# TensorE: the high-part multiplications of a group first, then the low-part ones

## The reference

```
inputs = emb[feature_ids] * feature_vals[:, :, None]          # (1024, 39, 16)
h = inputs
for i in range(3):
    x = einsum('bhd,bmd->bhmd', h, inputs).reshape(B, -1, 16)  # every h times every field
    x = relu(einsum('bcd,oc->bod', x, Ws[i]) + bs[i])          # 200 outputs
    h, direct = (x[:, :100], x[:, 100:]) if i != 2 else (None, x)
    finals.append(direct)
d = relu(relu(inputs.reshape(B, -1) @ dnn_W0.T + dnn_b0) @ dnn_W1.T + dnn_b1)
out = concat(sum(finals, axis=-1), d) @ fc_W.T + fc_b + sum(bias_emb[feature_ids] * feature_vals)
```

## Time and profile before

| | |
|---|---|
| median of 3 runs | 2750.92 us (2747.41 to 2753.69) |
| profiled execution, its own time | 2752.34 us |
| its span, first to last instruction | 2750.5 us |
| TensorE matmul busy | 2649.5 us, 96% of the span |
| TensorE weight load busy | 2640.2 us, 96% |
| VectorE, GpSimd, ScalarE busy | 83%, 82%, 67% |

### The profile page before, as it was taken

The page is one execution under the profiler, slowest core; times in us unless marked ns, Lnnn a source line. Parts: engine busy times, 40 slices in busy tenths (PEclk is TensorE's granted clock), DMA queues, the critical chain, the costliest instruction groups (busy, mean ns, idle before and its releaser), DMA issues.

```text
span 2750.5 us, 66670 instructions
## 1 busy us (share of the span) xinstructions
PE 2649.5 (96%) x17928; PEld 2640.2 (96%) x17928; DVE 2285.0 (83%) x4584; ACT 1834.6 (67%) x4776; POOL 2249.6 (82%) x1912
## 2 busy tenths in 40 slices
PE   0699999999999999999999999999999999999999
PEld 0599999999999999999999999999999999999998
DVE  2788888888888888888888888888888888888884
ACT  0576776766767667676777767677677766766663
POOL 6788888888888888888888888888888888877763
PEclk9799999999999999999999999999999999999999
DMA  8844545445444454544545455454554545545441
GB/s 149 199 124 123 133 126 130 124 118 144 116 133 125 118 149 112 136 121 122 146 111 138 120 131 137 114 136 118 138 131 118 133 117 140 129 117 136 111 115 51
DMA packets 199914, 349.82 MB, mean 127 GB/s; under 512 B 66632, under 2 KB 118697, under 8 KB 199615
## 3 DMA queue, kind: packets, MB, share of 16 engines
q1 hardware_dynamic: 185782, 342.81, 45.6%
q0 software_dynamic: 10496, 2.88, 3.1%
q10 hardware_dynamic: 3464, 2.68, 0.3%
HBM read 344.29 MB, written 14.17 MB: 130 GB/s over the span
## 4 chain that ended last, share of the span: by engine, by line
PE 94%; POOL 2%; SPq 2%; DVE 1%; issue 1%; DMA 1%; ACT 0%; POOLq 0%; ACTq 0%; DVEq 0%
PE acc L642 61%; PE acc L643 28%; PE acc L667 2%; POOL raw L498 1%; PE hrep L678 1%; DVE W L1061 0%; SPq L319 0%; DMA odd<-lin 0%; PE acc L742 0%; PE acc L743 0%; PE acc L744 0%; SPq L309 0%; DMA raw<-table,idx 0%; PE hrep L764 0%; PE hrep L766 0%
## 5 line engine op out<-in xcount | busy, mean ns | idle before, releaser
L642 PE MATMUL acc<-W,xhi_d 128*128 128x400 f32 x5632 | 1732.4, 367 | 17.2 <-DVE xlo_d L1087 10.6
L643 PE MATMUL acc<-W,xlo_d 128*128 128x200 f32 x5632 | 1434.9, 255 | 0.0
L1087 DVE TENSOR_TENSOR xlo_d<-prod_d,xhi_d 128x512 fp32r<-128x512 f32 (+1 forms) x1536 | 983.9, 641 | 205.1 <-ACT xhi_d L819 147.2
L1079 DVE TENSOR_TENSOR prod_d<-hrep,xrep 128x512 f32<-128x512 f32 (+1 forms) x1536 | 1039.0, 677 | 105.8 <-issue 27.7
L548 POOL TENSOR_TENSOR xlo_p<-prod_p,xhi_p 128x512 fp32r<-128x512 f32 (+1 forms) x768 | 953.8, 1242 | 181.3 <-ACT xhi_p L813 135.6
L642 PEld LDWEIGHTS acc<-W,xhi_d 128*128 128x128 f32 x5632 | 1059.9, 188 | 20.1 <-DVE xlo_d L1087 12.9
L643 PEld LDWEIGHTS acc<-W,xlo_d 128*128 128x128 f32 x5632 | 1078.4, 191 | 0.0
L819 ACT ACTIVATE xhi_d<-prod_d 128x512 fp32r<-128x512 f32 (+1 forms) x1536 | 885.1, 577 | 222.6 <-PE acc L643 199.8
L642 PE MATMUL acc<-W,xhi_p 128*128 128x400 f32 x2944 | 917.2, 363 | 12.9 <-POOL xlo_p L548 12.9
L542 POOL TENSOR_TENSOR prod_p<-hrep_s,xrep 128x512 f32<-128x512 f32 x512 | 665.9, 1301 | 161.3 <-ACT hrep_s L856 108.5
L643 PE MATMUL acc<-W,xlo_p 128*128 128x200 f32 x2944 | 751.7, 255 | 0.0
(11 more groups left out here) (92 smaller groups left out, 927.1 us busy)
## 6 DMA issues: line engine op xcount, KB each, us to landing
xrep<-xs SPq DMA_DIRECT2D x384, 384.0 KB
l0x<-xs SPq DMA_DIRECT2D x378, 136.5 KB
xrep<-xs SPq DMA_DIRECT2D x384, 128.0 KB
xrep<-xs SPq DMA_DIRECT2D x128, 336.0 KB
xrep<-xs SPq DMA_DIRECT2D x128, 64.0 KB
l0x<-xs SPq DMA_DIRECT2D x378, 19.5 KB
lin<-w SPq DMA_DIRECT2D x8, 750.0 KB
raw<-table,idx POOLq DMA_INDIRECT x328
```

Source lines behind the costliest of these rows:

```text
L642: pe.matmul(bank[:, 0:2 * OUTS], hi, w, start=first, stop=last, skip_group_check=True)
L643: return pe.matmul(bank[:, 0:OUTS], lo, w[:, 0:OUTS], start=False, stop=last, skip_group_check=True)
L1079: nc.vector.tensor_tensor(to, h, xrep[:, (par + layer - 1) % 2, a:a + count, :], ALU.mult).then_inc(s_prod_d, 1)
L1087: op = nc.vector.tensor_tensor(xlo_d[:, slot, 0:split], bank[:, 0:split], xhi_d[:, slot, 0:split].bitcast(F32), ALU.subtract)
```

## The change

Within a group, TensorE first multiplies by the high parts of all its tiles, then by the low parts of all that have one. The waits, the signals, the operands, the columns and the number of instructions stay as they were. Before, a group of four ran high, low, high, low, high, low, high, low; now high four times, then low four times. The helper `split_tile` is gone.

```
@@ multiply, TensorE @@
+                split = [t for t in tiles if layer == 0 or t != LAST_T]
                 for n, t in enumerate(tiles):
                     w = W[:, COL0[layer] + t * 2 * OUTS:COL0[layer] + (t + 1) * 2 * OUTS]
-                    hi, lo = hi_ring[:, slot, n * P:(n + 1) * P], lo_ring[:, slot, n * P:(n + 1) * P]
-                    start, end = first and n == 0, last and t == tiles[-1]
-                    if layer > 0 and t == LAST_T:
-                        mm = pe.matmul(bank[:, 0:2 * OUTS], hi, w, start=start, stop=end,
-                                       skip_group_check=True)
-                    else:
-                        mm = split_tile(bank, hi, lo, w, start, end)
+                    pe.matmul(bank[:, 0:2 * OUTS], hi_ring[:, slot, n * P:(n + 1) * P], w, start=first and n == 0,
+                              stop=last and t == tiles[-1], skip_group_check=True)
+                for n, t in enumerate(split):
+                    w = W[:, COL0[layer] + t * 2 * OUTS:COL0[layer] + t * 2 * OUTS + OUTS]
+                    mm = pe.matmul(bank[:, 0:OUTS], lo_ring[:, slot, n * P:(n + 1) * P], w, start=False,
+                                   stop=last and t == split[-1], skip_group_check=True)
                 mm.then_inc(done, 1)
```

More of the change, by code:

```diff
@@ L640, in _ @@
         def _(pe):
-            def split_tile(bank, hi, lo, w, first, last):
-                pe.matmul(bank[:, 0:2 * OUTS], hi, w, start=first, stop=last, skip_group_check=True)
-                return pe.matmul(bank[:, 0:OUTS], lo, w[:, 0:OUTS], start=False, stop=last, skip_group_check=True)
             def multiply(i, kind, g):
```

## The result

The changed kernel takes 2756.61 us (median of 22 runs, 2750.34 to 2761.36), the kernel before 2750.76 us beside it. The ratio is 1.0018 (95% interval 1.0011 to 1.0024): slower by 5 to 6 us (3.0 to 6.6 by the interval), at the edge of what can be measured, where 31 us less were forecast. That is 0.6 us above the range that was to hold 8 in 10. The profiled execution's span is 2754.3 us against 2750.5.

The account below looks back on a forecast made before the run. TensorE was taken to bound the kernel. Savings of 0.016 us per group of four, 0.012 per three and 0.007 for the last-tile groups make 0.259 a step; 124 steps save 32 us: 2720 us, range 2700 to 2741 (8 in 10: 2696 to 2756).

Parts of the forecast that it names:

- the price of low after low: In a group's run of lows, each interval goes at the pace of loads, 0.1085 us; four make 0.434 us.
- take-up: A high after a low waits for its load, then takes up its weights; paid once a group instead of four times.
- The transposes' 0.110: Four transposes, loads of 128 columns, stood 0.11 us apart; taken as the pace of a chain of loads.
- The second term: Second high in a group, after the first: 0.176 us, taken from the place like it at line 667.
- the first high, taken at 0.185: First high of each group: 0.185 us from load to load, as in every pair of the order before.
- The dense layers' 0.181: 17 steps of same-shape matmuls in the dense layers, 0.181 us each; used for a group's third and fourth highs.
- Rival 1: Each instruction costs its own in either order (low 0.112 us, high 0.181): no change, 2751 us; chance 0.20.
- Rival 2: Loads of lows drawn ahead by more than one, lows at 0.092 us: about 160 us less, 2590; chance 0.03.
- Rival 3: Additions to the same columns wait for each other: slower above 0.112 us a low, 2819 at 0.125; chance 0.11.
- The cover of 13%: VectorE and GpSimd have some 13% of their time left, so they can supply a TensorE 1.2% quicker.

Follow-up runs that it names:

- the run with other columns: Changed kernel, but low products of every second tile of a group added to columns 200 to 399 of the bank: 2754.62 us, ratio to before 1.0010.
- 4.6% less time: Changed order with lows kept as bfloat16 and eight of the 18 groups taking lows first: 2623.37 us, ratio 0.9537 to the kernel before.
- the grouped kernel: Changed order (highs first, then lows) with low products kept as bfloat16 and multiplied by high weights read as bfloat16: 2662.24 us, ratio 0.9677 to before.
- two halves of one change: New order only in the three groups of three tiles, ratio to before 1.0014; only in the 15 groups of four, 1.0007.

## Why the prediction was wrong

**What held.** TensorE sets the time; its waits hardly changed (1.5 us against 2.0 in the loop); the other engines had room; what a low matmul waits for is the load of the next tile.

**The step that failed** is the price of low after low: "in a chain of lows each load can start as the one before it ends, and only the chain's pace counts; the take-up is paid once in a group instead of four times". There is no take-up that a chain saves. I took the interval from start to start of two loads, 0.107 us (0.1085 in the sum), as what a load occupies, and called the 0.004 us left to 0.112 something else. The loads' own lengths, which I had in the profile and did not use, tell otherwise. Groups of weight loads before, with the mean in ns after the comma:

```profile
L643 PEld LDWEIGHTS acc<-W,xlo_d 128*128 128x128 f32 x5632 | 1078.4, 191 | 0.0
L642 PEld LDWEIGHTS acc<-W,xhi_d 128*128 128x128 f32 x5632 | 1059.9, 188 | 20.1 <-DVE xlo_d L1087 12.9 <-DVE xhi_d L1090 6.5 <-issue 0.5
```

The load that comes 0.107 to 0.108 us behind another is 0.003 us longer, as if it started a little before it could go on. From end to end the interval is some 0.111 us. In the chain of the changed kernel the loads of the lows come as far apart (separate views; a row of two starts with its first):

```profile
1400.66 0.30 PEld L666 LDWEIGHTS acc<-W,xlo_d 128*128 128x128 f32 x2
1400.77 0.30 PEld L666 LDWEIGHTS acc<-W,xlo_d 128*128 128x128 f32 x2
1400.88 0.19 PEld L666 LDWEIGHTS acc<-W,xlo_d 128*128 128x128 f32 x1
```

The next load, of a high, starts at 1401.00: 0.34 us for three intervals, where the forecast had 0.326. With 0.112 and 0.181, four of each make 1.172 us, measured 1.17. Against the forecast's 1.157 that is 0.015 more, of which 4 × (0.112 − 0.1085) = 0.014 is the price of the lows. The transposes' 0.110 was no help either: their loads are shorter, 140 ns at line 752 of the kernel before against 191.

**The second term** was the high after a first high. At line 667 it showed 0.176, and I carried it to 18 places a step. It belonged to those two places. It was 0.005 us too low, which the first high, taken at 0.185, nearly made up for. In the changed kernel the second high of a group of four goes on after 0.18 us (start 1400.12, the third 1400.30, the fourth 1400.48):

```profile
1400.12 0.52 PE L662 MATMUL acc<-W,xhi_d 128*128 128x400 f32 x2
1400.30 0.53 PE L662 MATMUL acc<-W,xhi_d 128*128 128x400 f32 x2
1400.48 0.34 PE L662 MATMUL acc<-W,xhi_d 128*128 128x400 f32 x1
```

The dense layers' 0.181, seventeen steps long, was the row to trust.

**Rival 1**, each instruction costs its own, is what happened, with both numbers that it named (0.112 and 0.181), and 0.020 us a step on top. 127 × 0.020 is 2.5 us of the 5 to 6 us measured (interval 3.0 to 6.6). The stretch at half clock would add 1.6, but the kernel before has such stretches too, and two profiles of one kernel reach the last transpose 3 to 4 us apart: where the rest comes from stays open. It had a chance of 0.20 and ought to have had more: the forecast stood on differences of 0.004 us between rows that are printed to 0.01.

**Rival 2**, all loads hidden: not seen, in the rows read a load is at most one matmul ahead. **Rival 3**, additions to the same columns: no cost, by the run with other columns (20.207 us a step against 20.206). The cover of 13% in the other engines was real: with 4.6% less time TensorE still waits for them only 2.8 us between 200 and 2500 us.

## What to carry to other kernels

Where every matmul has a load of its own, write down for each matmul the longer of its streaming and the load beside it; reordering changes the sum only if it changes which load lies beside which matmul. So ask first whether the loads differ. With equal loads the order was worth nothing here; with a cheaper kind for the lows it decided between 3% less and 5% more. An effect that rests on a few nanoseconds between rows of different kinds of instructions should be forecast as no change.

## What the runs showed of the hardware

A load of 128 float32 columns is hidden behind a matmul of 400 columns and costs 0.112 us behind one of 200 or of 104; one of 64 columns lets the matmul of 200 go at 0.092 us. A matmul of 400 columns takes 0.181 us and not the 0.167 of its columns. A bfloat16 load was not started beside a float32 matmul (0.17 us idle before it), a float32 load beside a bfloat16 matmul was (at 1401.75 us in the grouped kernel, with the last low). The granted clock of TensorE fell from 2.4 to 1.2 GHz for some 3 us at a time behind waits of 2.1 to 2.3 us, in either order, and not behind each. Steps of the loop repeated to 0.001 us between two executions in two kernels, while two halves of one change gave 0.014 and 0.034 us and both together 0.020: no run here shows why.
